# Windowed attention of a Trainium2 kernel: from 32-row look-back on 128-row tiles to 64-query blocks of 96 keys, in couples of head pairs

## The reference

```python
WINDOW, QK_SCALE = 32, 8.0
def attn_layer(x, Wqkv, qs, ksc, Wo):
    q, k, v = heads(x @ Wqkv)
    q, k = l2norm(q) * qs, l2norm(k) * ksc
    q = q * cos * scale + rotate_half(q) * sin * scale
    k = k * cos / scale + rotate_half(k) * sin / scale
    # local_attention: query i sees key j with i - 32 <= j <= i
    sim = where(mask, -max, q @ k.T * QK_SCALE)
    return softmax(sim) @ v @ Wo
for i in range(6):
    x = attn_layer(shift_tokens(x), ...) + x
    x = ffn_layer(shift_tokens(x), ...) + x     # layer norm, gated GELU, 341 wide
```

## Time and profile before

| what | us |
|---|---|
| median of 3 runs | 6041.95 |
| lowest, highest | 6040.45, 6043.06 |
| the profiled execution | 6046.58 |
| its span in the profile | 6044.8 |
| PE busy | 5374.6 (89%) |
| DVE busy | 4235.2 (70%) |
| ACT busy | 3913.8 (65%) |
| POOL busy | 2701.1 (45%) |

### The profile page before, as it was taken

The page is one execution under the profiler, slowest core; times in us unless marked ns, Lnnn a source line. Parts: engine busy times, 40 slices in busy tenths (PEclk is TensorE's granted clock), DMA queues, the critical chain, the costliest instruction groups (busy, mean ns, idle before and its releaser), DMA issues. The chain is left out here.

```text
span 6044.8 us, 121573 instructions
## 1 busy us (share of the span) xinstructions
PE 5374.6 (89%) x41154; PEld 3795.8 (63%) x41154; DVE 4235.2 (70%) x16128; ACT 3913.8 (65%) x11510; POOL 2701.1 (45%) x2580
## 2 busy tenths in 40 slices
PE   7885799999999999997499999999999999697989
PEld 5674466666666666665256666666666666464678
DVE  4453788888888888885488888888888887454522
ACT  2211588888888888884178888888888888222333
POOL 0000556566565665652166566565565655230000
PEclk9996899999999999998599999999999999697999
DMA  0000000000000000000000000000000000000000
GB/s 11 22 1 3 22 1 12 9 12 9 5 12 6 12 9 12 8 1 4 21 1 11 8 3 12 9 12 9 7 10 6 12 8 1 5 2 4 2 29 8
DMA packets 30964, 53.45 MB, mean 9 GB/s; under 512 B 7688, under 2 KB 17168, under 8 KB 29712
## 3 DMA queue, kind: packets, MB, share of 16 engines
q1 hardware_dynamic: 30352, 45.66, 2.4%
HBM read 44.60 MB, written 1.05 MB: 8 GB/s over the span
## 5 line engine op out<-in xcount | busy, mean ns | idle before, releaser
L1791 PE MATMUL bank<-wA,next_rowT 128*128 128x512 f32 x2304 | 1217.0, 630 | 206.7 <-DVE turnB L2141 88.6
L1995 ACT ACTIVATE pairs<-pairs,negmax 128x128 f32<-128x128 f32 (+1 forms) x3072 | 1236.9, 418 | 8.0 <-DVE negmax L2102 7.0
L1972 POOL TENSOR_TENSOR turnA<-raw,ropes 128x512 f32<-128x512 f32 x768 | 969.1, 1272 | 152.6 <-ACT raw L2019 123.8
L2102 DVE CUSTOM_DVE_ANT_0 pairs<-bank,bands,big 128x128 f32<-128x128 f32 (+1 forms) x3072 | 940.6, 362 | 62.9 <-PE bank L1720 59.4
L1979 POOL TENSOR_TENSOR qk<-turnA,turnB 128x512 f32<-128x512 f32 x768 | 976.4, 1272 | 6.4 <-DVE turnB L2141 6.4
L1951 POOL COPY spread<-recip 128x256 f32<-128x256 f32 x768 | 305.6, 398 | 1262.7 <-DVE recip L2111 1256.9
L1791 PEld LDWEIGHTS bank<-wA,next_rowT 128*128 128x128 f32 x2304 | 370.8, 191 | 689.1 <-DVE turnB L2141 286.3
L2002 ACT ACTIVATE pairsT<-bank 128x512 f32<-128x512 f32 x768 | 465.9, 607 | 303.7 <-PE bank L1733 303.4
L1995 ACT ACTIVATION_READ_ACCUMULATOR pairs<-pairs,negmax 128x1 f32 x3072 | 624.7, 203 | 0.0
L285 POOL TENSOR_TENSOR rstd<-vareps,neg_half 128x2 f32<-128x2 f32 x56 | 39.0, 696 | 1288.4 <-DVE vareps L256 892.3
L2141 DVE TENSOR_TENSOR turnB<-bank,ropes 128x512 f32<-128x512 f32 x768 | 522.4, 680 | 0.0
(11 more groups left out here) (313 smaller groups left out, 11261.8 us busy)
## 6 DMA issues: line engine op xcount, KB each, us to landing
wA<-in_wt_wqkv SPq DMA_DIRECT2D x72, 256.0 KB, 2.8
wB<-in_wt_wo SPq DMA_DIRECT2D x12, 512.0 KB, 3.5
wC<-in_wt_w SPq DMA_DIRECT2D x12, 341.0 KB, 2.9
wD<-in_wt_w SPq DMA_DIRECT2D x12, 192.0 KB, 2.3
big<-in_e_up SPq DMA_DIRECT2D x1, 2048.0 KB
big<-in_e_down SPq DMA_DIRECT2D x1, 2048.0 KB
scl<-in_wt_scales SPq DMA_DIRECT2D x12, 128.0 KB, 3.3
X<-in_x SPq DMA_DIRECT2D x8, 128.0 KB, 2.3
```

Source lines behind the costliest of these rows:

```text
L1791: pe.matmul(side_bank(i)[:, :], c.next_rowT[:, t * P:(t + 1) * P], wqkv[:, k * 512:(k + 1) * 512], start=True, stop=True).then_inc(s.chunk ...
L1972: g.tensor_tensor(c.turnA[:, m % 2, :].rearrange("p (h d) -> p h d", h=8), c.raw[:, m % 4, :].rearrange("p (h d) -> p h d", h=8), cos, ALU ...
L1995: last = a.activation(tile, tile, ACT.Exp, scale=-1.0, bias=c.negmax[:, 2 * p + side, t:t + 1], accum_out=c.pair_sums[:, p % 4, t, side:si ...
L2102: last = v.tensor_tensor_reduce(c.pairs[:, 2 * (p % 4) + side, AT[t]:AT[t] + SPAN[t]], c.bank[side][:, AT[t]:AT[t] + SPAN[t]], c.bands[:, ...
```

## The change

Queries are taken in blocks of 64 with 96 keys (the block and the 32 keys before it; the first block of a row has 64), and two pairs of heads, a *couple*, share one step. For a couple in an even slot, scores are 16 matmuls of 64 queries, 64 rows deep, each in one corner of the array, two heads by two blocks. The maximum and the exps take 96 columns in place of 128 or 160. A pair's probabilities are turned by four transposes of 96 rows. Values are weighed in odd slots by 16 matmuls a couple, 96 deep, 64 queries by 64 columns, in two column halves, so that the context comes out in token order. There the scale is one DVE multiplication with a broadcast reciprocal (128x512, `dve_scale_ctx`); then PE turns the context with four transposes (`pe_turn_ctx`) and ACT copies it. The POOL spread, the turned shares and their copies, and the stream transposes are gone. The values of a turn, now in one tile, are laid on 96 partitions by six DMAs a turn (`sp_values`), from SBUF to SBUF, on SP's queue; the weight loads move into `sp_window` between them. `dve_roots` goes from slot 2 to slot 3, the statistics with it, behind the copy of a key quarter and the scaling of a couple. The gates of the feed-forward part come ahead of the scores of T+1 in slot 6, and `dve_last_hidden` later in slot 7. The mask is loaded by a DMA at the start in place of being built by POOL, and two PSUM areas and the first rows of the value tiles are zeroed there.

```diff
-DVE_RSQRT_SLOTS = {2: 0, 6: 1}
+DVE_RSQRT_SLOTS = {3: 0, 6: 1}
...
+        def pe_scores(pe, T, n):
             j = T % 2
...
+            pe.wait_ge(s.qT_copied, T * 4 + n + 1)
+            pe.wait_ge(s.kT_copied, T * 4 + n + 1)
+            if T > T0 or n > 0:
+                pe.wait_ge(s.negmax_ready, T * PAIRS + 2 * n)
+            for e in range(2):
+                for t in range(HALVES):
+                    for w in range(2):
+                        q0 = t * P + w * BLOCK
+                        k0 = max(q0 - WINDOW, 0)
+                        keys = q0 + BLOCK - k0
+                        at = (2 * e + t + 1) * BLOCK_KEYS - keys
+                        for side in range(2):
+                            q, k = [x[j][DH * side:DH * side + DH, 2 * n + e, :] for x in (qT, kT)]
+                            last = pe.matmul(c.bank[side][w * BLOCK:(w + 1) * BLOCK, at:at + keys], q[:, q0:q0 + BLOCK],
+                                             k[:, k0:k0 + keys], start=True, stop=True, skip_group_check=True)
             last.then_inc(s.scores_ready, 1)
...
+            for g in range(4):
+                last = pe.transpose(probs_bank(p)[0:BLOCK_KEYS, g * P:(g + 1) * P], pairs[:, p % 4, g, :], c.ident[:, :])
...
+        def pe_weigh(pe, T, n):
+            pe.wait_ge(s.probsT_ready, T * PAIRS + 2 * n + 2)
+            pe.wait_ge(values_laid[n // 2], VALUE_PARTS * (T + 1))
+            if T > T0 or n > 0:
+                pe.wait_ge(s.ctx_ready, T * COUPLES + n)
+            for e in range(2):
+                for t in range(HALVES):
+                    for side in range(2):
+                        at = ((2 * e + t) * 2 + side) * DH
+                        for w in range(2):
+                            turned = c.probsT[0:BLOCK_KEYS, e, (2 * side + t) * P + w * BLOCK:(2 * side + t) * P + (w + 1) * BLOCK]
+                            last = pe.matmul(c.bank[4][w * BLOCK:(w + 1) * BLOCK, at:at + DH], turned,
+                                             values[n // 2][0:BLOCK_KEYS, 2 * t + w, 4 * (n % 2) + 2 * e + side, :],
+                                             start=True, stop=True, skip_group_check=True)
             last.then_inc(s.ctx_in_psum, 1)
+        def pe_turn_ctx(pe, T, n):
+            pe.wait_ge(s.ctx_scaled, T * COUPLES + n + 1)
+            for m in range(4):
+                last = pe.transpose(c.bank[4][:, m * P:(m + 1) * P], scaled[:, m * P:(m + 1) * P], c.ident[:, :])
+            last.then_inc(s.ctxT_in_psum, 1)
...
+            for slot in range(PAIRS):
+                n = slot // 2
+                if slot % 2 == 0:
+                    if slot < 6:
+                        pe_scores(pe, T, n + 1)
+                    pe_turn_probs(pe, T, slot + 1)
+                    if n >= 1:
+                        pe_turn_ctx(pe, T, n - 1)
+                    elif has_turn(T - 1):
+                        pe_turn_ctx(pe, T - 1, COUPLES - 1)
+                    if slot == 0 and following:
+                        pe_xT(pe, T + 1)
+                    if slot == 6 and has_turn(T - 2):
+                        pe_gates(pe, T - 2, (s.qT_copied, (T + 1) * 4 + (1 if following else 0)))
+                    if slot == 6 and following:
+                        pe_scores(pe, T + 1, 0)
+                else:
+                    pe_weigh(pe, T, n)
...
+                if slot == 5 and has_turn(T - 2):
                     pe_turn_normed(pe, T - 2)
+                if slot % 2 == 1 and n + 1 < COUPLES:
+                    pe_turn_probs(pe, T, slot + 1)
+                elif slot % 2 == 1 and following:
+                    pe_turn_probs(pe, T + 1, 0)
...
+        def dve_scale_ctx(v, T, n):
+            v.wait_ge(s.recip_ready, T * COUPLES + n + 1)
+            v.wait_ge(s.ctx_in_psum, T * COUPLES + n + 1)
+            shares = c.recip[:, 0, 8 * (n % 2):8 * (n % 2) + 8].unsqueeze(2).broadcast_to((P, 8, DH))
+            v.tensor_tensor(scaled[:, :].rearrange("p (n d) -> p n d", n=8), c.bank[4][:, :].rearrange("p (n d) -> p n d", n=8),
+                            shares, ALU.mult).then_inc(s.ctx_scaled, 1)
...
         def dve_window(v, T):
             following = has_turn(T + 1)
...
+            for slot in range(PAIRS):
+                n = slot // 2
+                if slot == 6 and following:
                     dve_copy_k(v, T + 1, 0)
...
+                if slot == 7 and has_turn(T - 1):
                     dve_add(v, T - 1)
...
+                if slot % 2 == 0:
+                    dve_recip(v, T, n)
+                if following:
+                    for m in DVE_ROTATE_SLOTS.get(slot, ()):
+                        dve_rotate(v, T + 1, m)
+                if slot == 3:
+                    dve_copy_k(v, T, COPY_LATE_QKT_SLOTS[slot])
+                if slot % 2 == 0:
+                    for e in range(2):
+                        if n + 1 < COUPLES:
+                            dve_negmax(v, T, 2 * n + 2 + e)
+                        elif following:
+                            dve_negmax(v, T + 1, e)
+                else:
+                    dve_scale_ctx(v, T, n)
+                if slot == 0:
+                    dve_copy_k(v, T, COPY_LATE_QKT_SLOTS[slot])
+                if slot == 1 and has_turn(T - 3):
+                    dve_ff_add(v, T - 3)
+                if slot == 7 and has_turn(T - 2):
                     dve_last_hidden(v, T - 2)
...
+                if slot == 3 and has_turn(T - 2):
                     dve_ff_stats(v, T - 2)
                 if following:
...
+                    dve_prepare(v, T + 1, slot)
+                elif slot == 3:
                     dve_roots(v, ss[:, ff_var], rs[(T + 1) % 2][:, ff_var])
...
+                if slot == 4 and has_turn(T - 2):
                     dve_ff_normalise(v, T - 2, rs[(T + 1) % 2][:, ff_var])
...
+                if slot == 7:
                     if has_turn(T - 2):
                         dve_first_hidden(v, T - 2)
...
+        def sp_values(sp, q, part):
+            sp.wait_ge(s.chunk_copied, q * N_CHUNKS + (6, 12)[part])
+            if q > T0:
+                sp.wait_ge(s.ctx_in_psum, q * COUPLES - (2, 0)[part])
+            src, out, done = V[:, :, 8 * part:8 * part + 8, :], values[part], values_laid[part]
+            sp.dma_start(out[WINDOW:BLOCK_KEYS, 0:4:2, :, :], src[0:BLOCK, :, :, :]).then_inc(done, 16)
+            sp.dma_start(out[0:BLOCK_KEYS, 1:4:2, :, :], src[WINDOW:P, :, :, :]).then_inc(done, 16)
+            sp.dma_start(out[0:WINDOW, 2, :, :], src[P - WINDOW:P, 0, :, :]).then_inc(done, 16)
...
+        def sp_window(sp, T):
+            if T - 2 > T0 and starts_layer(T - 2):
+                sp_last_weights(sp, T - 2)
+            turning = has_turn(T + 2) and starts_layer(T + 2)
+            if turning:
+                sp_scales(sp, T + 2)
+                sp_projections(sp, T + 2, WEIGHT_ORDER[0:3])
+            if has_turn(T + 1):
+                sp_values(sp, T + 1, 0)
+            if turning:
+                sp_projections(sp, T + 2, WEIGHT_ORDER[3:6])
+            if T > T0 and starts_layer(T):
+                sp_out_weights(sp, T)
+            if has_turn(T + 1):
+                sp_values(sp, T + 1, 1)
+            if T - 1 > T0 and starts_layer(T - 1):
+                sp_ff_weights(sp, T - 1)
```

More of the change, by code:

```diff
@@ L131, in allocate @@
     c.pair_sums = sb("pair_sums", [P, 4, HALVES, 2])
[L132 removed]
+    c.shares = sb("shares", [P, 2 * S])
+    c.late_values = sb("late_values", [P, 4, NH // 2, DH])
     c.recip = sb("recip", [P, 2, 32])
[L134 removed]
     c.ctx = sb("ctx", [P, HALVES, D])
@@ L1647, in windowed_transformers @@
     wqkv_loaded = [sem(name + "_wqkv_loaded" + str(k)) for k in range(CHUNKS)]
+    values_laid = [sem(name + "_values_laid" + str(n)) for n in range(2)]
     step = Count(steps)
@@ L1652, in windowed_transformers @@
     vn, tn = HALVES * NH * DH, 8 * S
-    V = (c.V, c.big[:, 0:vn].rearrange("p (t h e) -> p t h e", t=HALVES, h=NH))
+    V = c.V
+    values = (c.big[:, 0:vn].rearrange("p (m h e) -> p m h e", m=4, h=NH // 2), c.late_values)
+    pairs = c.pairs[:, :, :].rearrange("p a b -> p (a b)")[:, 0:16 * BLOCK_KEYS].rearrange("p (n g k) -> p n g k", n=4, g=4)
+    scaled = c.shares
     qT = (c.qT, c.big[:, vn:vn + tn].rearrange("p (k s) -> p k s", k=8))
@@ L1726, in pe_turn_probs @@
             pe.wait_ge(s.probs_ready, T * PAIRS + p + 1)
-            if T * PAIRS + p > T0 * PAIRS:
-                pe.wait_ge(s.probsT_ready, T * PAIRS + p)
-            for side in range(2):
-                probs, out = c.pairs[:, 2 * (p % 4) + side, :], c.bank[2][:, S * side:S * side + S]
-                pe.transpose(out[:, 0:P], probs[:, 0:P], c.ident[:, :])
-                last = pe.transpose(out[:, P:2 * P], probs[:, P + WINDOW:2 * P + WINDOW], c.ident[:, :])
-            last.then_inc(s.probsT_in_psum, 1)
@@ L2082, in act_window @@
+                if slot == 3:
+                    act_copy_q(a, T, COPY_LATE_QKT_SLOTS[slot])
+                p = slot + 2
```

(35 more changed lines are left out.)

299 lines of the change are left out of this document (100 added, 199 removed).

## The result

The changed kernel takes 6340.98 us (median of 4 runs, 6340.22 to 6341.84) against 6041.61 before: 1.0495 times as long, interval 1.0477 to 1.0514, so 299 us slower. The forecast was 6365, in a range of 6170 to 6560, and slower with a chance of 0.82.

What follows compares the result with a forecast made beforehand. PE was taken to bound the kernel, 42.3 of 44.62 us a turn. The profiled 6046.6 + 239 (new order's waits, less saved PE work) + 83 (clock) = 6369, 4.6 above the median, so about 6365; range 6170 to 6560.

Steps and rivals of the forecast that it cites:

- The chain: One turn followed from chunk 0 through PE, DVE and ACT: 47.2 us against 44.62, +2.6 a turn, +239 us.
- The cause: Slots 2 to 4: DVE's statistics and roots, behind the key quarter's copy, delay chunk 8's rotation; PE waits 2.2 us.
- The clock: Waits before chunks 8 and 10 may bring 3.3 us of half clock; half the turns, 0.9 a turn, +83 us.
- The scores: PE's scores of a couple: 32 records in four corners, 0.86 plus 0.21, 1.07 us.
- 27 ns a record: PE's matmuls in parts of the array: time per record, from eight-record groups starting 0.22 us apart.
- entry and exit: PE's scores: 0.21 us beyond the columns' time, left from 0.49 of 0.70 in the kernel before.
- the weighing: PE's weighing of a couple: 32 records of 64 columns in two halves, 0.88 plus 0.15, 1.03 us.
- the corners: Rival on PE's scores: corners run only two at a time, 1.4 us a turn, 127 us, 6490; chance 0.13.
- the issue: Rival on PE's short records: issue, not columns, sets the pace, 430 us more, about 6470; chance 0.02.
- The transfers: Six DMAs a turn that lay the values, wanted over 20 us after issue: cost 0, even at three times 2.8 us.
- step 8: End of the turn: next quarters turned and copied, scores, context, ACT's copies (1.9) ahead of next chunk 0, reaching 47.2 us.

Runs made afterwards that it cites:

- Experiment 4: Kernel before with only its statistics and roots moved from slot 2 to slot 3, behind the key quarter's copy: 6326.53 us, 1.0471 times the kernel before.
- experiment 1: Changed kernel with DVE's statistics and roots back in slot 2, ahead of the key quarter's copy: 6168.45 us.
- experiment 5: Changed kernel with the first scores of the next turn again ahead of the gates in slot 6: 6236.77 us.
- experiment 2: Changed kernel with the weighing of the third couple (slot 5, ahead of chunk 10) done three times over: 6321.55 us.
- experiment 3: Changed kernel with the values laid on 96 partitions by DMA for the first turn of each windowed transformer only: 6332.25 us.
- experiment 9: Changed kernel with both orders undone, plus chunks 8 and 9 squared before slot 4's exps, layer-norm subtraction later, chunk 0's queries copied before the context: 6008.26 us.
- experiment 10: On experiment 9, four DVE maxima moved from ahead of the roots to behind the key quarter's copy, chunk 6 copied before that pair's exps: 6037.03 us.
- experiment 7: Changed kernel with both orders undone, plus the first weighing moved from the start of slot 1 to the end of slot 0, ahead of chunk 0: 6107.59 us.

## Why the prediction was right

- **The chain.** Its steps from the start of chunk 0, forecast and measured in the turn shown above: end of the key quarter's transposes 13.65, 13.5 (2020.31 + 1.09); chunk 8 20.1, 19.9; chunk 10 25.6, 25.4; turns of slot 6 29.4, 30.3; gates 32.0, 33.0 (29.2 and 31.9 in the turn of 1623.57, whose chunks 10 and 11 run at the full clock). Chunk 0 of the next turn: 47.2 without the clock, and 47.27 in turns that it does not lengthen; 48.1 with the 0.9 a turn counted for it, against 47.94 on average. Waits 2.2, 2.3 and 1.3 were forecast, 1.88, 2.12 and 1.23 are there, the second in 6 of 21 turns only.
- **The cause.** Experiment 4 puts the roots' place alone into the kernel before and gets 284 of the 299 us; experiment 1 takes it out of the changed one and gets 172 back, experiment 5 the gates' place and gets 104. With both undone the usual turn is 44.40, under the 44.63 of before, so the geometry costs nothing by itself. The cause named is shown, not only argued.
- **The clock.** I took the low stretch in half of the turns, 0.9 a turn. It follows in nearly every turn, 83 of 86, but costs time in 43 of them, since it mostly falls on chunks 8 and 9 and hides in the wait for chunk 10. That half of the turns pay is luck; the prediction did not see the hiding. Slot 5 from chunk 10 to the next turns is 4.92 us there (2033.29 to 2038.21) and 3.77 in the turn of experiment 2 without one (2030.02 to 2033.79, where the turns of slot 6 start in it): 1.15, the price in such a turn, where 1.7 was counted. On average the clock was worth 47.94 - 47.27 = 0.67 a turn, less than the 0.9, and the rest of the change from turn to turn, 2.64, is the 2.6 forecast for the chain. The clock is most of the 24 us by which the time came out under the forecast.
- **The scores.** 0.82 a couple in place of 1.07: the term was sized by 27 ns a record, and by columns it comes out. The first block of a row has 64 keys, so a record has 88 columns on average and not 96, 8 x 88 x 0.86 = 0.61, and with the 0.21 for entry and exit 0.82. The 27 ns is a mean over parts that work side by side, not a distance that records keep. The Trainium skill ("TensorE: Matmul & The Clock Gate", section "Wait — 56ns, not 53.3ns?") says that matmuls start no closer than about 25 ns, however short. For matmuls in different corners the trace does not agree, and it decides: four records start within 0.05 us, in the timeline from 2014.55 to 2014.60, where starts 25 ns apart would spread over 0.075.

```profile
2014.56 0.31 PE L1723 MATMUL bank<-kT,qT 64*64 64x64 f32 x4
```

  The four corners do work side by side, and the weighing, 1.09, is near the 1.03 counted. The rivals of the corners and of the issue are out.
- **The transfers.** Counted at nothing; experiment 3 gives 9 us of 6341. A landing takes 4.1 us, more than the 2.8 of the earlier trace rows, and nobody waits for it.
- **What was missing.** The wait for chunk 0, 1.24, stood in step 8 only as a list of copies, and I took POOL's hold on a small DVE operation for a detail. It is 1.1 us a turn before, 1.5 in experiments 1 and 9 and 2.0 in experiment 10, for whoever puts the roots beside POOL's rotations.

## What to carry to other kernels

When work is taken off the busiest engine, follow one period of the pipeline from a fixed instruction to its next instance, through every engine in program order: what stands behind a late arrival decides, not the sum of the engine's work. A long block with early inputs belongs ahead of the instruction that waits late. Undo one reordering at a time on both geometries: here the order cost 284 us with the old one, and a better order, with one copy moved to ACT, made the new one 3.4% faster than before. And where the clock can fall, compare turns and not only times: an edit can shorten the chain and lose it again to the clock (experiment 9), or seem to cost on the chain what the clock costs (experiment 7).
